# Four output matmuls instead of eight, biases carried in the projections, and products moved to GpSimd

## The reference, cut to what matters

```
x = x + L0_conv(ln_c(x))      # attention over the 16 images, 8 heads of 16
   zn = layernorm(z);  q, k, v = zn @ Wq, Wk, Wv;  g = sigmoid(zn @ Wg + bg)
   att = softmax over j of q_i . k_j / 4;  o = (att @ v) * g;  out = o @ Wo + bo
t = t + L0_ffn(ln_t(t))       # 8 experts, the best 2 of each token
   p = top2(softmax(x @ router_w + router_b)), normalised
   out = sum over the 2 of p * (x @ expert_w + expert_b)
x = x + L1_conv(ln_c(x))      # expand to 2 x 64, scan over rows a
   s = 0.9 s + 0.1 gating;  out = (primary * sigmoid(s)) @ W_con + b_con
x = x + L1_ffn(ln_t(x))       # each of 32 experts picks its 8 best tokens of an image
```

## Time and profile before

| what | value |
|---|---|
| median of 3 runs | 2711.42 us (2711.4 to 2712.73) |
| the profiled execution, its own time | 2704.94 us |
| its span, first to last instruction | 2703.1 us |
| mean granted TensorE clock | 0.937 of full |
| busy: PE, DVE, ACT, POOL | 2383.0, 2245.5, 1657.3, 2107.5 us |
| idle of PE ahead of L701, by POOL `split_conv` | 146.6 us |
| HBM traffic | 55.56 MB read, 50.33 MB written |

### The profile page before, as it was taken

How to read it: one execution, slowest core, us unless ns; L and a number is a source line. 1 busy time by engine, 2 the same in 40 slices (tenths; PEclk the granted TensorE clock), 3 DMA queues, 4 the chain that set the end, 5 groups by cost and what they waited for, 6 DMA issues and landing times. The chain is left out here.

```text
span 2703.1 us, 127455 instructions
## 1 busy us (share of the span) xinstructions
PE 2383.0 (88%) x45291; PEld 1715.2 (63%) x45291; DVE 2245.5 (83%) x8757; ACT 1657.3 (61%) x3077; POOL 2107.5 (78%) x3098
## 2 busy tenths in 40 slices
PE   4999999999999999999999999999999999997368
PEld 3666666666666666666666666666666666664258
DVE  3688898898888988889888898888988889886626
ACT  3556666666666666666666666666676666663330
POOL 3677788888888888888888888888888888885310
PEclk9888899999999999999999999999999999996579
DMA  1001111111111111111111111111111111111579
GB/s 22 9 18 22 21 22 20 22 20 21 22 19 23 20 21 22 20 23 20 21 22 20 22 20 21 21 20 23 19 21 22 20 23 20 21 21 16 175 280 373
DMA packets 263185, 107.28 MB, mean 40 GB/s; under 512 B 251284, under 2 KB 253882, under 8 KB 259003
## 3 DMA queue, kind: packets, MB, share of 16 engines
q1 hardware_dynamic: 260831, 101.54, 16.0%
q10 hardware_dynamic: 2268, 4.57, 0.5%
HBM read 55.56 MB, written 50.33 MB: 39 GB/s over the span
## 5 line engine op out<-in xcount | busy, mean ns | idle before, releaser
L516 ACT ACTIVATE kT<-shared,b_k,quarter 128x512 f32<-128x512 f32 x512 | 364.3, 789 | 0.0
L835 DVE TENSOR_TENSOR yg<-shared,gates 128x512 f32<-128x512 f32 x512 | 344.7, 685 | 22.9 <-PE shared L646 22.5
L932 DVE TENSOR_REDUCE mixed<-yg 128x256 f32<-128x2048 f32 x128 | 285.5, 2231 | 0.3
L460 POOL TENSOR_TENSOR probs<-weights,own_den 128x1024 f32<-128x1024 f32 x128 | 247.3, 1932 | 17.0
L645 PE MATMUL shared<-w_expert_hi,tT 128*128 128x512 f32 x512 | 260.5, 509 | 0.0
L653 PE MATMUL shared<-w_o,ogT 128*128 128x64 f32 x2048 | 255.2, 279 | 4.6 <-DVE ogT L975 4.4
L653 PEld LDWEIGHTS shared<-w_o,ogT 128*128 128x128 f32 x2048 | 245.3, 196 | 15.5 <-DVE ogT L975 9.5
L701 PE MATMUL shared<-ident,split_conv 128*128 128x128 f32 x512 | 100.0, 328 | 146.6 <-POOL split_conv L427 146.6
L546 ACT COPY lT<-shared 64x512 f32<-64x512 f32 x128 | 74.1, 579 | 222.5 <-PE shared L674 222.5
L646 PE MATMUL shared<-w_expert_lo,tT 128*128 128x512 f32 x512 | 204.5, 399 | 0.0
L731 PEld LDWEIGHTS o_bank<-probsT,v_sb 32*32 32x32 f32 x16384 | 165.4, 104 | 59.9 <-issue 54.8
(11 more groups left out here) (200 smaller groups left out, 7139.0 us busy)
## 6 DMA issues: line engine op xcount, KB each, us to landing
x_in<-in_x SPq DMA_DIRECT2D x1024, 16.0 KB, 1.7
x_scratch<-x SPq DMA_DIRECT2D x1024, 16.0 KB, 1.5
normalized_x_scratch<-norm_pick SPq DMA_DIRECT2D x1024, 16.0 KB, 1.4
xa<-normalized_x_scratch SPq DMA_DIRECT2D x8, 1024.0 KB, 8.1
xc<-normalized_x_scratch SPq DMA_DIRECT2D x8, 1024.0 KB, 12.5
out_x<-xc SPq DMA_DIRECT2D x16, 512.0 KB, 5.3
xc<-x_scratch SPq DMA_DIRECT2D x4, 1024.0 KB, 8.4
xb<-x_scratch SPq DMA_DIRECT2D x4, 1024.0 KB, 17.0
```

What stands on the lines that cost most here:

```text
L460: g.tensor_tensor(probs[:], weights[:].unsqueeze(2).broadcast_to([P, 32, 2, 16]), own_den[:].unsqueeze(3).broadcast_to([P, 32, 2, 16]), AL ...
L516: ins = s.activation(kT[:, h, :], bk("k"), ACT.Identity, bias=b_k[:, h:h + 1], scale=quarter[:, h:h + 1])
L835: v.tensor_tensor(yg[:, t], bk(y).rearrange("p (d e) -> p d e", e=NE), gates[:, t, :].unsqueeze(1).broadcast_to([P, D, NE]), ALU.mult).the ...
L932: v.tensor_reduce(mixed[:], yg[:], AX.X, ALU.add).then_inc(s_mixed, 1)
```

## The change

- The values are written to PSUM with all even-parity columns first (columns 0 to 127 of a bank) and all odd ones behind. ScalarE scales the even part with a mask of 1 or 0 per row (`oA`, into `o_even`); VectorE masks the odd part and adds (`og`, one instruction, into `o_own`); GpSimd multiplies by the gate (`ogm`). `att_out` then needs four matmuls, with Wo undoubled.
- Biases: the 64th normalised channel, which follows from the other 63, is replaced by a constant 1 in the attention and the expert input. The projections for q, k, gate, v, router and experts carry the bias in that row, so the bias matmuls of the experts and of v go. `bo` and `b_con` come in through two bf16 bias matmuls of 256 columns (`att_out`, `scan_out`); ScalarE copies (`xkeep`, `x2keep`) take the place of GpSimd's `xbo` and `x2bc`.
- The centring of the conv and pick layernorms moves into centred weights: GpSimd's `sub_conv` and `sub_pick` go.
- `gated` becomes one GpSimd product of 512 elements a row, from a tanh that ScalarE first writes out per half (`ema1`); `gates` and `lgm` move from VectorE to GpSimd, `top2` and `lg` to ScalarE. The router runs in two rounded parts.
- The pooled phase subtracts the mean of the pooled row: three ScalarE instructions in place of one, four times.
- All orders, lags and PSUM banks are new; there are thirteen stages, eight columns unrolled. Setup is rearranged.

```diff
-    1: "r1_att sub_att pow_att mul_att lo_att rnd_att zT qA km0 att_t q k v ag_att",
...
-    6: "sub_conv mul_conv lo_conv x2bc rnd_conv cT exA conv_t expand scan",
...
+    1: "sub_att r1_att pow_att mul_att lo_att rnd_att zT km0 gateA km1 qA att_t k gate q scores",
...
+    3: "ogm gp1 att_out x1 st_ffn ag_ffn",
...
+TURNS = ["v", "y2", "scan_out", "ffn_t", "conv_t", "att_t", "route", "expand", "k", "gate", "att_out", "pick",
...
-                    if runs(i, q, "sub_pick"):
-                        z = par(q, "sub_pick")
-                        pool.wait_ge(s_agg["pick"], at(i, q, "sub_pick"))
-                        wait(pool, filled["pick_t"], at(i, q, "sub_pick", 2))
-                        wait(pool, s_n3_store[z], stored(i, q, "sub_pick", 2))
-                        g.tensor_tensor(norm["pick"][z][:], x3[z][:], mv["pick"][z][:, :, 0:1].broadcast_to([P, QT, D]),
...
-                    if runs(i, q, "xbo"):
-                        z = par(q, "xbo")
-                        pool.wait_ge(s_centered["att"], at(i, q, "xbo"))
-                        wait(pool, drained["att_out"], at(i, q, "xbo", 2))
-                        g.tensor_tensor(x_bo[z][:], x_in[z][:], bo_rows[:].unsqueeze(1).broadcast_to([P, QT, D]), ALU.add).then_inc(s_xbo, 1)
...
+                    if runs(i, q, "mul_pick"):
+                        z = par(q, "mul_pick")
+                        pool.wait_ge(s_rstd["pick"], at(i, q, "mul_pick"))
+                        wait(pool, filled["pick_t"], at(i, q, "mul_pick", 2))
+                        wait(pool, s_n3_store[z], stored(i, q, "mul_pick", 2))
+                        g.tensor_tensor(norm["pick"][z][:], x3[z][:], rstd["pick"][z][:, 1, :].unsqueeze(2).broadcast_to([P, QT, D]),
+                                        ALU.mult).then_inc(s_norm["pick"], 1)
...
+                    if runs(i, q, "gates"):
+                        pool.wait_ge(s_grec, at(i, q, "gates"))
+                        for t in range(QT):
+                            wait(pool, drained[f"y{t}"], at(i, q, "gates", 1))
+                        g.tensor_tensor(gates[:], sel[:], gden[:].unsqueeze(2).broadcast_to([P, QT, NE]), ALU.mult).then_inc(s_gates, 1)
...
+                    if runs(i, q, "gated"):
+                        z = par(q, "gated")
+                        pool.wait_ge(s_emat, column(i, q, "gated") + 1)
+                        wait(pool, filled["scan_out"], at(i, q, "gated", 2))
+                        half = slice(z * 32, (z + 1) * 32)
+                        g.tensor_tensor(gated[z][:].rearrange("p a (h n) -> p a h n", h=2), ema_own[:, half],
+                                        prim[:, half, :].unsqueeze(2).broadcast_to([P, A // 2, 2, 8]), ALU.mult).then_inc(s_gated, 1)
...
+                    if runs(i, q, "ogm"):
+                        z = par(q, "ogm")
+                        pool.wait_ge(drained["values"], at(i, q, "ogm"))
+                        pool.wait_ge(s_gp1, at(i, q, "ogm"))
+                        wait(pool, filled["att_out"], at(i, q, "ogm", 1))
+                        by_tile = lambda a: a.rearrange("p (t g i) -> p g t i", g=4, i=32)
+                        g.tensor_tensor(by_tile(ogT[:]), o_own[:].rearrange("p (g t i) -> p g t i", g=4, i=32), by_tile(gT[z][:]),
+                                        ALU.mult).then_inc(s_og, 1)
...
+                    if runs(i, q, "lgm"):
+                        pool.wait_ge(s_top, at(i, q, "lgm"))
+                        wait(pool, s_ratio, at(i, q, "lgm", 1))
+                        g.tensor_tensor(lgm[:], lg[:], top8[:, :, 0:1].broadcast_to([P, QT, NE]), ALU.subtract).then_inc(s_diff, 1)
...
-                            ins = s.activation(kT[:, h, :], bk("k"), ACT.Identity, bias=b_k[:, h:h + 1],
-                                               scale=quarter[:, h:h + 1])
+                            ins = s.mul(kT[:, h, :], bk("k"), quarter[:, h:h + 1])
...
+                    if par(q, "ema1") == 1 and runs(i, q, "ema1"):
+                        act.wait_ge(s_tanh, column(i, q, "ema1") + 1)
+                        wait(act, s_gated, at(i, q, "ema1", 2))
+                        for h in range(2):
+                            ins = s.activation(ema_own[:, :, h, :], ema_t[:], ACT.Identity, bias=half_of[:, h:h + 1], scale=half_of[:, h:h + 1])
+                        ins.then_inc(s_emat, 1)
...
+                    if runs(i, q, "xkeep"):
+                        z = par(q, "xkeep")
+                        act.wait_ge(s_centered["att"], at(i, q, "xkeep"))
+                        wait(act, drained["att_out"], at(i, q, "xkeep", 2))
+                        s.copy(x_keep[z][:], x_in[z][:]).then_inc(s_xkeep, 1)
...
+                    if runs(i, q, "oA"):
+                        act.wait_ge(s_o, at(i, q, "oA"))
+                        wait(act, drained["values"], at(i, q, "oA", 1))
+                        s.mul(o_even[:].rearrange("p (g x) -> p g x", g=4), o_bank[:, :, 0:P], odd_even[:, 0:1]).then_inc(s_oeven, 1)
...
-                        t_.matmul(bk(y), ones3[:], bias3[:], start=True, stop=False)
-                        t_.matmul(bk(y), tT[z][:, tile(t)], w_expert_hi[:], start=False, stop=False)
+                        t_.matmul(bk(y), tT[z][:, tile(t)], w_expert_hi[:], start=True, stop=False)
...
+                        t_.matmul(bk("scan_out")[:, 0:QT * D], ones3[:], b3[:, 1, :], start=True, stop=False)
...
+                            t_.matmul(bk("route")[:, cols_], tT[z][:, tile(t)], w_router_hi[:], start=True, stop=False)
+                            ins = t_.matmul(bk("route")[:, cols_], tT[z][:, tile(t)], w_router_lo[:], start=False, stop=True)
...
-                                ins = t_.matmul(bk("att_out")[:, t * D:(t + 1) * D], ogT[:, h, tile(t)], w_o2[:, h, :],
-                                                start=(h == 0), stop=(h == 1))
...
+                        pe.wait_ge(s_og, at(i, q, "att_out"))
+                        t_.matmul(bk("att_out")[:, 0:QT * D], ones3[:], b3[:, 0, :], start=True, stop=False)
+                        for t in range(QT):
+                            ins = t_.matmul(bk("att_out")[:, t * D:(t + 1) * D], ogT[:, tile(t)], w_oh[:],
+                                            start=False, stop=(t == QT - 1))
                         ins.then_inc(filled["att_out"], 1)
...
+                                    ins = t_.matmul(by_head(o_bank[k * 32:(k + 1) * 32, g])[:, :, t * 32:(t + 1) * 32],
+                                                    v_sb[z][g * 32:(g + 1) * 32, t, k * 32:(k + 1) * 32],
+                                                    pT[g * 32:(g + 1) * 32, k // 2, t, m:m + 2, :], tile_position=(g * 32, k * 32))
...
-                    if runs(i, q, "gated"):
-                        z = par(q, "gated")
-                        dve.wait_ge(s_emat, column(i, q, "gated") + 1)
-                        wait(dve, filled["scan_out"], at(i, q, "gated", 2))
-                        half = slice(z * 32, (z + 1) * 32)
-                        for h in range(2):
-                            rows = slice(h * D, (h + 1) * D)
-                            ins = v.scalar_tensor_tensor(gated[z][rows, :, h * 8:(h + 1) * 8],
-                                                         ema_t[rows, half, :], 1.0, prim[rows, half, :], ALU.add, ALU.mult)
-                        ins.then_inc(s_gated, 1)
...
-                        by_group = lambda a: a.rearrange("p (t g i) -> p g t i", g=4, i=32)
-                        for h in range(2):
-                            o = o_bank[:, :, 0:QT * 64].rearrange("p g (t h i) -> p g t h i", h=2, i=32)[:, :, :, h, :]
-                            ins = v.tensor_tensor(by_group(ogT[:, h, :]), o, by_group(gT[z][:]), ALU.mult)
-                        ins.then_inc(drained["values"], 1)
...
+                        dve.wait_ge(s_oeven, at(i, q, "og"))
+                        wait(dve, s_og, at(i, q, "og", 1))
+                        by_group = lambda a: a.rearrange("p (g x) -> p g x", g=4)
+                        v.scalar_tensor_tensor(by_group(o_own[:]), o_bank[:, :, P:2 * P], odd_even[:, 1:2], by_group(o_even[:]), ALU.mult,
+                                               ALU.add).then_inc(drained["values"], 1)
...
-                    s.mul(pooled[:, gr, :], banks[2][:, gr * D:(gr + 1) * D], prec[:, gr:gr + 1]).then_inc(s_pool_cp, 1)
+                    s.activation(pooled[:, gr, :], banks[2][:, gr * D:(gr + 1) * D], ACT.Copy, scale=prec[:, gr:gr + 1],
+                                 accum_out=pooled_sum[:, gr:gr + 1]).then_inc(s_pooled, 1)
+                    act.wait_ge(s_pooled, 2 * gr + 1)
+                    s.mul(pooled_sum[:, gr:gr + 1], pooled_sum[:, gr:gr + 1], -1.0 / D).then_inc(s_pooled, 1)
+                    act.wait_ge(s_pooled, 2 * gr + 2)
+                    s.activation(pooled[:, gr, :], pooled[:, gr, :], ACT.Identity, bias=pooled_sum[:, gr:gr + 1]).then_inc(s_pool_cp, 1)
```

(66 more changed lines are left out.)

767 lines of the change are left out of this document (365 added, 402 removed).

## The result

The changed kernel takes 2473.07 us (median of 4, 2472.13 to 2474.82), the kernel before 2711.41 us beside it: ratio 0.9121, 95% interval 0.9105 to 0.9137. Forecast were 2511 us, 2440 to 2665. The profiled execution spans 2470.3 us.

A forecast was written before the change was run, and what follows sets the result against it. Three nearly equally loaded engines waiting for each other bound the kernel. Span 2703.1 - 183.6 (loop) - 26.4 (ramp, drain) + 7.4 (extra stage) + 2.0 (pooled phase) = 2502.5, plus 1.84 and 6.5: forecast 2511 us, range 2440 to 2665.

The forecast's parts named there:

- GpSimd's base: GpSimd's time per loop slot without its waits, issue gaps left in: 16.95 us before, forecast 16.85 after the change.
- the `pow`: GpSimd's pow_pick in the loop: forecast to fall by 0.17 us, from 1.185, once VectorE's gated no longer runs beside it.
- The allowance of 0.25 us for waits: Loop slot: 0.25 us of waiting added to GpSimd's forecast 16.85 us, giving a slot of 17.10 us.
- the ring: Loop: TensorE, GpSimd and VectorE, nearly equally loaded, wait for each other; slot 1.43 us above the fullest engine.
- The ring rival: Loop: waits above the fullest engine stay at 1.43 us; slot 18.28 us, time 2661 us; chance 0.17.
- The clock rival: TensorE in the loop: more idle time brings low-clock stretches oftener; slot 17.9 us, time 2613 us; chance 0.12.
- The slower rival: GpSimd's two new products cost far more than priced; at 2.5 us each, slot 19.53, time 2820 us; chance 0.11.
- the low half of its bounds: Price of each new 512-element GpSimd product: bounds 1.06 us low and 1.58 us high, 1.29 us taken.
- its base, counted as in the forecast: TensorE's time per loop slot without its waits, issue gaps left in: 17.32 us before, forecast 15.07 after.
- the 15.4: ScalarE's likely time per loop slot after the change, in us, with the two keeps at half; at most 16.06.
- at half: ScalarE's xkeep and x2keep, 256 elements each, priced at half of the 0.718 us upper price.
- the offset that I added from span to median: Added to the forecast span of 2502.5 us: 1.84 us to the execution's own time, 6.5 more to the runs' median.

The follow-up runs named there:

- the two further runs: Kernel before, ag_conv moved ahead of scan and lg, without five bias matmuls and half of og and att_out: 2674.47 us; kernel before, VectorE's slot-end steps reordered: 2915.46 us.

## Why the prediction was right, and where it was not

**The size of the slot: right, by its terms.** GpSimd's base was forecast at 16.85 us and is 17.06. The products, the `pow`, lgm and gates came as priced. Missing was 0.39 us at L371, of which smaller terms gave back 0.18: I wrote that the new products would be slowed only beside the scan, and did not ask which operation the new order puts beside it. The allowance of 0.25 us for waits was not needed, GpSimd has none. That the slot came out within 0.04 us (17.10 and 17.06) is luck: two errors nearly cancel. That GpSimd's work now sets the slot is shown by +1.44 for +1.29 of its work and +0.06 for over 2 us of TensorE's.

**The reason the ring would go: wrong.** "The load moves from three nearly equal engines to one" explained the waits by load. Without 2.49 us of TensorE's load the slot stayed at 18.76. What the runs show instead is waits laid by the order of steps: moving one step that needs nothing of its neighbours took 0.37 us off the slot and the wait at `rstd_conv` away. That closed chains make up all 1.8 us is read from the timelines only, not shown; the two further runs meant to show it missed. One chain was visible in the earlier trace rows: `rstd_conv` for `mv_conv` 155.3, `split_conv` 136.8, `lg` 117.0 are its three hops, and I read them as three symptoms.

**What opened the chains in the changed kernel** is seen in its trace, not tested apart. All four operations that leave GpSimd (2.94 us) stood on the piece from `r1_conv` to `split_conv`; `r1_conv` comes one slot later (its `ag_conv` ends at 1053.50 us, it starts at 1057.81, so 4.3 us to spare); `lg` has left VectorE, where it stood ahead of `ag_conv`. Which of these suffices is open.

**The ring rival** (18.28 us, 0.17) had the premise of my forecast, and falls with it. **The clock rival** (17.9 us, 0.12) did not come, although TensorE is idle 2.7 us a slot: granted clock in the loop is 0.98, and it was at the lower level for 71.7 us in 21 stretches there, against 112.6 us in 33 before (three slots in ten, not one in four). What it warned of came in the kernel before with both chains' steps moved, behind a wait of 1.26 us in each turn. The Trainium skill (TensorE: Matmul & The Clock Gate, HAM oscillation) warns of waits between bursts of matmuls; that run agrees, with 0.83, while the changed kernel with more idle time, in several shorter waits, keeps 0.98. **The slower rival** is refuted by 1.275 us a product, the low half of its bounds.

**Smaller terms.** `att_out` went from 1.95 to 1.11 us a slot (0.84 saved, 0.97 forecast), plus 0.21 for its bias. TensorE is idle 2.7 us a slot, 2.5 of it in waits for others (forecast near 2), and its base, counted as in the forecast, is 14.56 against 15.07: the three groups of transposes behind the old wait at L701 take 0.44 us less a slot, which I had not counted. ScalarE is busy 13.67, under the 15.4: `oA` came as priced (0.72), the two keeps took 0.42 and 0.41 (0.36 at half), the passes of `ema1` 0.81 each, above the 0.718 that I had called the most, and the masked keys fell from 0.789 to 0.695 us without their bias. Of the 38 us between forecast and time 28 lie outside the loop, 4 in it, and 5.6 in the offset that I added from span to median (8.3; it is 2.8). Outside the loop the start lost 5.7 us (forecast 0), the ramp 31.2 (18.2), the first stretch of drain 22.2 (8.3); the 12.7 us of the longer drain (forecast 7.4) and 1.4 of the pooled phase (2.0) were near.
